# SyncE asks for the weights of experts 1 to 3 ahead of, not behind, the softmax inverses in the last batch

## The reference

```
x = x + attention(layernorm(x), context)        # 16 heads, softmax over 375 context rows
h = layernorm(x)
p = softmax(h @ gate_w); keep the top 2 of 8, renormalised
y[e] = (silu(h @ gate_up_w[e][:, :512]) * (h @ gate_up_w[e][:, 512:])) @ down_w[e]
x = x + sum over the two chosen e of share[e] * y[e]
```

## Time and profile before

| | |
|---|---|
| median of 3 runs | 1529.89 us (1528.06 to 1531.57) |
| profiled execution, its own time | 1532.48 us |
| profiled execution, span of the core | 1530.5 us |
| PE busy | 1466.9 us, 96% |
| DVE, ACT, POOL busy | 947.6, 729.4, 548.1 us |
| attention, batch 31 | from about 1122 to 1180 us of the span |
| tiles of the experts on PE | from 1190 us to the end |

### The profile page before, as it was taken

How to read it: one execution, slowest core, us unless ns; L and a number is a source line. 1 busy time by engine, 2 the same in 40 slices (tenths; PEclk the granted TensorE clock), 3 DMA queues, 4 the chain that set the end, 5 groups by cost and what they waited for, 6 DMA issues and landing times. The chain is left out here.

```text
span 1530.5 us, 37348 instructions
## 1 busy us (share of the span) xinstructions
PE 1466.9 (96%) x11882; PEld 1294.5 (85%) x11883; DVE 947.6 (62%) x2580; ACT 729.4 (48%) x2030; POOL 548.1 (36%) x635
## 2 busy tenths in 40 slices
PE   6999999999999999999999999999974899999997
PEld 5788989988888888899888888888964788888886
DVE  5667777677767677776777776777655533333332
ACT  4555555555555555555555555555534222222222
POOL 3224333343433343333434333424247132332322
PEclk9999999999999999999999999999996899999999
DMA  6522222222222222222222232131036223333232
GB/s 177 150 67 70 72 66 76 67 70 65 76 68 93 85 71 70 68 73 67 70 67 74 69 95 87 38 97 33 28 105 222 53 49 53 50 51 52 48 55 25
DMA packets 101099, 113.73 MB, mean 74 GB/s; under 512 B 17244, under 2 KB 88140, under 8 KB 101068
## 3 DMA queue, kind: packets, MB, share of 16 engines
q1 hardware_dynamic: 88444, 96.43, 20.6%
q0 software_dynamic: 12144, 15.66, 6.3%
q10 hardware_dynamic: 480, 1.24, 0.3%
HBM read 61.37 MB, written 51.93 MB: 74 GB/s over the span
## 5 line engine op out<-in xcount | busy, mean ns | idle before, releaser
L797 ACT ACTIVATE prob<-bank,neg_max 112x375 f32<-112x375 f32 x512 | 298.5, 588 | 139.7 <-DVE neg_max L1061 139.7
L1061 DVE TENSOR_REDUCE neg_max<-bank 112x1 f32<-112x375 f32 x512 | 243.8, 538 | 17.4 <-PE bank L1299 17.3
L1309 PE MATMUL bank<-ident,prob 112*125 112x112 f32 x1536 | 216.0, 275 | 16.3 <-ACT prob L797 16.2
L1309 PEld LDWEIGHTS bank<-ident,prob 112*125 112x125 f32 x1536 | 197.0, 189 | 27.9 <-ACT prob L797 18.8
L736 POOL DMA_INDIRECT out<-y_out,dest_now x63 | 97.7, 1551 | 243.2 <-ACT y_out L889 218.1
L1333 PE MATMUL bank<-probT,V 125*64 125x112 f32 x3072 | 177.9, 265 | 2.7 <-DVE probT L1067 2.0
L1207 PE MATMUL bank<-Wgu,hT_h 128*128 x504 | 175.3, 429 | 1.6 <-DVE hT_l L1164 1.6
L1333 PEld LDWEIGHTS bank<-probT,V 125*64 125x64 f32 x3072 | 150.2, 138 | 29.2 <-issue 24.3
L925 DVE TENSOR_TENSOR K_l<-bank,K_h 128x376 fp32r<-128x376 f32 x256 | 140.3, 549 | 53.3 <-ACT K_h L757 46.6
L915 DVE COPY V<-bank 125x512 f32<-125x512 f32 x96 | 66.4, 691 | 137.4 <-PE bank L1271 134.4
L1185 DVE COPY hidT<-bank 128x512 f32<-128x512 f32 x63 | 43.7, 693 | 173.6 <-PE bank L1509 173.6
(11 more groups left out here) (174 smaller groups left out, 3504.2 us busy)
## 6 DMA issues: line engine op xcount, KB each, us to landing
bins<-pad_rows SPq DMA_DIRECT2D x29, 1032.0 KB, 5.9
inv_rows<-sums SPq DMA_DIRECT2D x126, 128.0 KB, 2.9
Wgu<-in_L_ffn_gate_up_w SPq DMA_DIRECT2D x8, 1024.0 KB, 7.2
h_in<-bins SPq DMA_DIRECT2D x63, 129.0 KB, 2.1
y_sb<-in_ctx SPq DMA_DIRECT2D x32, 187.5 KB, 2.7
y_sb<-in_ctx SPq DMA_DIRECT2D x62, 93.8 KB, 2.6
x_sb<-in_x SPq DMA_DIRECT2D x16, 224.0 KB, 2.9
x_res<-in_x SPq DMA_DIRECT2D x32, 112.0 KB, 2.4
```

The lines of the kernel that those rows point to most:

```text
L797: nc.scalar.activation(prob[:, j, :], S_ps[j][0:LQ, 0:LKV], ACT.Exp, bias=neg_max[:, j:j + 1], accum_out=row_sum[:, head // HB, head % HB: ...
L1061: nc.vector.tensor_reduce(neg_max[:, j:j + 1], S_ps[j][0:LQ, 0:LKV], AX.X, ALU.max, negate=True).then_inc(max_done, 1)
L1309: last = nc.tensor.transpose(S_ps[j][0:KR, t * LQ:t * LQ + LQ], prob[:, j, t * KR:t * KR + KR], ident[0:LQ, 0:LQ])
```

## The change

In batch 31, and nowhere else, SP first goes through the three loads of experts 1 to 3 with the semaphore waits that guard them, and only then through the spreading of the inverses of the first eight heads. The load of 3 MB of `Wd` stays behind the inverses. No instruction is added or removed.

```
                     if there(b + 2, STRIDE // P):
                         sp.wait_ge(prefilled[odd], 16 * (i + 1))
                         prefill(b + 2, odd)
-                    if there(b, B):
-                        spread_inverses(b, 0)
                     if known(i) and i == NP - 1 and odd:
                         sp.wait_ge(made, a.made(a.find(0, "q", 7)))
                         load_expert(sp, 1)
...
                         load_expert(sp, 2)
                         sp.wait_ge(made, a.n0 + len(a.items))
                         load_expert(sp, 3)
+                    if there(b, B):
+                        spread_inverses(b, 0)
+                    if known(i) and i == NP - 1 and odd:
                         sp.dma_start(Wd[:, early:E].rearrange("p e k n -> p (e k) n"),
                                      down_w[early:E].rearrange("e (k p) n -> p (e k) n", p=P)).then_inc(wd_in, 16)
```

## The result

The changed kernel takes 1519.33 us (median of 5 runs, 1518.95 to 1523.03), the kernel before 1530.44 us in the same series. The ratio, taken over all runs and not from the two medians, is 0.9935, with a 95% interval of 0.992 to 0.9951: 9.9 us faster (7.5 to 12.2). The forecast was 14.6 us. 0.9935 of the 1529.9 us from which it was made is 1519.9, just above its range of 1512.5 to 1519.5; the bare median lies just inside. The direction came out, and so did the end of the two waits that the change was to remove; about a third of the gain did not.

The account below looks back on a forecast made before the run. PE, busy 96% of the span, was taken as the bound, its 12.6 us standstill due to late loads. Terms 11.3 + 1.5 + 0.3 + 1.5 = 14.6 us took the median 1529.9 to 1515.3 us, range 1512.5 to 1519.5.

Parts of the forecast that it names:

- SP's queue: Batch 31: loads 1 to 3 issued at 1123.95, 1124.5 and about 1130.5; SP ready 3.5 us before the inverses.
- Rival C: SP held in issuing the store of the inverses: nothing won (1529.9 us) or slower; chance 0.03.
- Landing: Load 1 lands 6.5 us after issue, at 1130.5; load 3 at 1136, so ACT casts at 1136.1.
- rival B: The small store of the inverses waits for slow load 3: gain 9.1 us, time 1520.8; chance 0.08.
- DVE: Copies of the turned heads in batch 31 end at 1143.6 against 1154.93: 11.3 us sooner (10.9 to 11.7).
- the three signs: Wrong if L483 issues well after 1134.6, L989 waits far over 1.9 us for DMA, or tiles start under 11 us sooner.
- Rival A: The inverses' transpose (L977) on DVE is held under POOL's subtraction: 2.5 us lost, 1517.8; chance 0.12.
- PE's clock: Without the long standstill PE keeps the upper clock level after DVE's copies: 1.5 us gained (0 to 1.6).
- Rival D: PE's clock falls anyway in short idle gaps: gain 12.3 us, time 1517.6; chance 0.17.
- POOL and the last residual: Two terms: POOL's earlier end of splitting, 0.3 us (0 to 1.2), and the stretch to the last residual, 1.5 (0.3 to 2.4).
- Two waits, either of which holds PE: In batch 31 ACT and POOL both wait on one late group of loads, and either would hold PE.

Follow-up runs that it names:

- the marks late: Changed kernel with DVE's marks of batch 29 moved, in batch 31, from step 1 to step 2 behind two turned heads: ratio 0.9914, again 0.9923.
- without the subtraction: Changed kernel without POOL's subtraction for experts 1 and 2, their low parts left as raw weights: ratio 0.9895 to the kernel before.
- the quarters: Changed kernel with POOL's subtraction for experts 1 and 2 cut into four pieces: ratio 0.9901 to the kernel before, again 0.9915.
- that gap filled: Changed kernel with 28 identity turns on PE in step 2 of batch 31, before the exponentials are turned: ratio 0.9934 to the kernel before.

## Why the prediction was right or wrong

**SP's queue: right.** Counted from L483, the first load went 13.8 us sooner and the third 8.6, the wait on `made` ended 3.7 us ahead of the inverses, nothing behind it came late, and SP was not held in issuing. Rival C did not occur.

**Landing: right in kind, too cautious.** POOL found load 1 there when it came at 1128.94, at most 5.6 us after the issue, not 6.5; load 3 let ACT begin 0.9 us behind L483 instead of 1.5. POOL's splitting began 5.0 us ahead of L483 instead of 4.0. The slow landing of rival B did not occur.

**DVE: this step failed.** The forecast had the copies of the turned heads end 11.3 us sooner. From L483 they ended 12.40 us on instead of 20.36: 8.0 us sooner, 3.3 short, as much as the whole gap between 14.6 and 11.2; that the rest of the sum fits is luck, 1.1 too little from PE's clock and 1.1 too much behind it. The prediction named the hold, cited the rule, and reckoned with one instruction under the first subtraction, "and the maxima of step 2 behind it slip by 1.1 us, under ACT's own cast: the sum stays". It stopped at the first. An instruction that is let go at the end of POOL's one meets POOL's next, because POOL had 13.0 us of such work without a gap: 0.9, 1.6 and 4.3 us beyond the usual durations, 6.8 in all. The forecast's own places would have shown it. With POOL splitting from 1130.6 to 1143.5, as it reckoned, the scaling would be let go only at 1143.5 and the product with the inverses start at about 1145.4 instead of 1140.9 (an estimate, with the 1.9 us from one to the other that the trace after the change has): 4.5 us less, a sum near 10.

Measured, the maxima came 5.9 us later than before, counted from L483 (8.02 against 2.12). The cover, DVE's wait for the inverses, had been 1.88 us; the product with them started 3.9 us later than before (9.84 against 5.91), of which the forecast had 0.4. With the marks late, or without the subtraction, the copies ended 8.3 and 8.9 us behind L483, where the forecast had 9.1.

None of the three signs that the prediction named for being wrong appeared: L483 went on time, the product with the inverses did not wait for its DMA, and the last residual, with the tiles behind it, came 11.8 us sooner by the times of the two traces. They looked at SP and the landings. What told was the place of that product, 1143.8 instead of 1140.9, and the granted clock around 1144.

The rule was that of the Trainium skill, "SBUF — State Buffer", section "Who interferes with whom": the loser of the shared port blocks until the other's instruction is over. The trace agrees with it three times, and so do the quarters, where no hold outlasts one POOL instruction. Its word that an operation with one input outside the two-port modes is free was right of the transpose: L978 took 0.21 us within POOL's first subtraction. Rival A did not occur.

**PE's clock: the term came to 0.4 instead of 1.5.** From the end of DVE's copies to the scores of step 3 the changed kernel gained 0.4 us (8.35 less 7.96): the pause ahead of the product shrank by 0.5, and the product took 2.51 us where 1.40 was reckoned. Rival D named this outcome. In this kernel the clock fell in the 3.71 us for which DVE's hold made PE stand, and in the one trace with that gap filled the clock stayed up and 1.4 us of the way came back. But the hold is not all of it: without that long gap the product of step 2 ran at the higher level with the marks late (1.37 us), and at the lower one in their second trace (2.48), without the subtraction (2.38) and with both traces of the quarters (2.46 and 2.51). So the upper level was not to be counted on, and this part of rival D stood.

**POOL and the last residual: undervalued by 1.1.** These two terms, 1.8 together, came to 2.9. PE's last product (0.8) and an unhindered widening on DVE (0.8) gave more than half of it, the gate and the last projection 1.4, the way from the exponentials to the inverses, in which PE had waited for POOL, 0.3, and the slower scores of step 3 took 0.4 back. First before, then after:

```profile
1164.14 2.17 PE L1333 MATMUL bank<-probT,V 125*64 125x112 f32 x24
```

```profile
1153.41 0.43 DVE L972 COPY inv_wide<-inv_sum 112x512 f32<-112x512 f32 x1
1154.49 1.37 PE L1334 MATMUL bank<-probT,V 125*64 125x112 f32 x24
```

**Two waits, either of which holds PE: right in kind.** Load 3 alone gained nothing, loads 1 and 2 alone the larger part, and this because DVE's hold had made ACT's wait cheap.

## What to carry to other kernels

When work is brought forward on an engine that shares a port with another, lay its whole new stretch over the other's timeline and go through every instruction there, not up to the first that is caught; small ones are let in one at a time between the large ones, and several can be caught in a row. Move them out of the stretch, or cut the large instructions. And where two engines wait for late transfers, the wait that the profile shows is only the one that ends last: here it was ACT's, and taking it away alone gained nothing.

## What the runs showed of the hardware that was not expected

DVE's comparison of 16 elements was held by a cast of POOL (1.80 us after the change) and by its subtraction alike (1.11 us at 1168.59 before it). Under POOL's `tensor_scalar` a product of the same size was not: in the changed kernel `picked` started inside that instruction in 29 of 32 batches and took 0.16 to 0.17 us in 28 of them, 0.40 in one.

The clock does not fall at the same place in each execution. With the marks late, PE stood 2.04 us and kept the higher level in one trace; with no subtraction it stood 2.13 us, and the product behind it ran at 0.50. In the trace of the filled gap the granted clock was at 0.50 from 1138 to 1141 with PE busy throughout, 2 us after a stop of 0.93 us, and the product of step 1 took 2.51 us instead of 1.40. It fell at that point in two more of the 14 traces, the second with the marks late (2.51 us) and that of the same edit on the kernel before (2.19 us); the other 11 have the same stop and keep 1.00. The window in the trace of the filled gap:

```profile
1138.00:1139.00 1.00, 1.00 (x12) 0.86 (x12) 0.82 (x4) 0.59 (x3) 1.00 (x1) 0.50 0.16 62
```

What decides this stays open. The two traces with the marks late are 2.3 us apart in their way.
